# A four-layer graph network on one core: part of the last edge stage's gathers moved to TensorE

## What is computed

```python
def layer_norm(x): return (x - x.mean(-1)) / sqrt(x.var(-1) + 1e-5)
h = maximum(layer_norm(x), 0.0)              # 6250 x 128
h = h @ W
loops = arange(6250)                         # one more self edge per node
src, dst = concat([src, loops]), concat([dst, loops])
deg  = segment_sum(ones, dst)
dinv = rsqrt(deg)
agg  = segment_sum(h[src] * (dinv[src] * dinv[dst])[:, None], dst) + bias
y = relu(layer_norm(agg) * gamma + beta)
out = y + x_before_the_layer
```

## Time and profile before

| | us |
|---|---|
| median of 3 runs | 9720.56 |
| lowest and highest run | 9702.98, 9722.01 |
| span of the profiled execution | 9708.2 |
| fourth edge stage, first to last gather issued | 7626.5 to 9638.9 |

### The profile page before, as it was taken

The page is one execution under the profiler, slowest core; times in us unless marked ns, Lnnn a source line. Parts: engine busy times, 40 slices in busy tenths (PEclk is TensorE's granted clock), DMA queues, the critical chain, the costliest instruction groups (busy, mean ns, idle before and its releaser), DMA issues. The chain is left out here.

```text
span 9708.2 us, 131917 instructions
## 1 busy us (share of the span) xinstructions
PE 5236.0 (54%) x29478; PEld 4578.8 (47%) x29478; DVE 6385.8 (66%) x17574; ACT 1742.2 (18%) x3229; POOL 7212.1 (74%) x6460
## 2 busy tenths in 40 slices
PE   2334343435555555555555588888888444444443
PEld 2333333334445444555545477777777433333333
DVE  4767677776777777666666688888888533333334
ACT  2222222222222222111111111111111200000001
POOL 4777777772888888888888477777777577777775
PEclk6555555556555555555555699999999655555555
DMA  6554554442777667777777422222222212222221
GB/s 154 127 127 116 129 131 117 113 115 65 111 112 111 110 109 110 109 109 111 112 111 111 104 57 56 56 57 56 56 57 56 54 53 53 53 53 53 53 53 52
DMA packets 1095241, 861.72 MB, mean 89 GB/s; under 512 B 408856, under 2 KB 931359, under 8 KB 1094342
## 3 DMA queue, kind: packets, MB, share of 16 engines
q0 software_dynamic: 386880, 427.12, 25.7%
q1 hardware_dynamic: 677244, 314.33, 14.3%
q10 hardware_dynamic: 30652, 115.04, 3.6%
HBM read 706.10 MB, written 149.64 MB: 88 GB/s over the span
## 5 line engine op out<-in xcount | busy, mean ns | idle before, releaser
L1291 POOL DMA_INDIRECT sums<-sumrows,index x1612 | 2520.9, 1564 | 666.2 <-issue 326.6
L675 POOL DMA_INDIRECT rows<-table,index x1612 | 1610.3, 999 | 598.6 <-issue 484.9
L1628 POOL DMA_INDIRECT rows<-table,index x1612 | 1522.6, 945 | 570.5 <-issue 490.7
L1432 POOL DMA_INDIRECT rows<-table,index x1612 | 1546.6, 959 | 512.2 <-issue 393.6
L1686 PE MATMUL psS<-hot,rows 128*128 128x128 f32 x3224 | 824.8, 437 | 1207.8 <-issue 1148.3
L1686 PEld LDWEIGHTS psS<-hot,rows 128*128 128x128 f32 x3224 | 717.8, 328 | 1314.8 <-issue 1270.5
L1259 PE MATMUL psX<-same,hotW 128*128 128x128 f32 x3224 | 810.1, 430 | 975.2 <-DVE hotW L1162 974.6
L1661 DVE TENSOR_TENSOR ACC<-ACC,psS 128x128 f32 x1612 | 465.7, 289 | 1201.6 <-PE psS L1686 1088.3
L1259 PEld LDWEIGHTS psX<-same,hotW 128*128 128x128 f32 x3224 | 698.3, 319 | 1103.1 <-DVE hotW L1162 1102.8
L1268 PE MATMUL psV<-win,mix 128*128 128x129 f32 x3224 | 797.2, 424 | 346.6 <-ACT mix L1225 340.7
L1523 PEld LDWEIGHTS psS<-hot,mid 128*128 128x128 f32 x6448 | 869.9, 196 | 38.1 <-issue 4.9
(11 more groups left out here) (303 smaller groups left out, 9532.9 us busy)
## 6 DMA issues: line engine op xcount, KB each, us to landing
win<-table SPq DMA_DIRECT2D x1612, 64.5 KB
srow<-src_f SPq DMA_DIRECT2D x403, 256.0 KB, 3.6
rows<-table,index POOLq DMA_INDIRECT x4836, 2.5
HN<-rel_f ACTq DMA_DIRECT2D x102, 512.0 KB
relB<-rel_f ACTq DMA_DIRECT2D x102, 512.0 KB, 4.5
er<-limbs SPq DMA_DIRECT2D x1632, 3.0 KB
sums<-sumrows,index POOLq DMA_INDIRECT x1612
ACC<-edge_marks SPq DMA_DIRECT2D x204, 96.0 KB
```

The source lines that it names most:

```text
L675: nc.gpsimd.indirect_dma_start(out=rows[:, r, k, :], out_offset=None, in_=table0[:, :], in_offset=bass.IndirectOffsetOnAxis(ap=index[:, n ...
L1291: nc.gpsimd.indirect_dma_start(out=sums1[u][:, :], in_=sums[:, s, u, :], in_offset=None, compute_op=ALU.add, out_offset=bass.IndirectOffse ...
L1432: nc.gpsimd.indirect_dma_start(out=rows[:, n % R, u, :], out_offset=None, in_=table2[:, :], in_offset=bass.IndirectOffsetOnAxis(ap=index[: ...
L1628: nc.gpsimd.indirect_dma_start(out=rows[:, n % R, u, :], out_offset=None, in_=table3[:, :], in_offset=bass.IndirectOffsetOnAxis(ap=index[: ...
```

## The change

The last BACK = 35 of the 403 groups are no longer gathered by GpSimd. GpSimd gathers the FRONT = 368 groups ahead of them. For the other 35, TensorE selects the source rows out of SBUF by a product with one-hots:

- The rows in `own` are split into three bf16 numbers each (`limbs`, 49 blocks of 128 x 384), high, middle and low part, by ScalarE (L1688, L1691, L1698) and VectorE (`less`, `least`), before ScalarE scales `own`.
- SyncE broadcasts a back group's 512 source numbers to all partitions (`names`), and ScalarE rewrites them as 16-bit integers (`short`).
- For each of the 49 blocks VectorE compares `short` with the block's node numbers (`picks`, L1754): one `tensor_scalar` of 128x512, 16-bit integers to a bf16 one-hot, in a ring of 9 (`pick`).
- TensorE multiplies the one-hots of four tiles by the block's limbs (`gather`, L1827): four matmuls of 384 columns per block, summed over the 49 blocks in four PSUM banks (`psG`). ScalarE copies the sums to `rowsL` (L1710, 128x1536), and TensorE makes the tile sums of a back group with three bf16 matmuls per tile (L1815).
- A back group's 49 blocks are spread over ten front groups (EACH = 10, from group 9 on): 4 or 5 blocks after each group's own matmuls. Group 359 closes the last one; eight front groups follow.
- A group's four sums now share one PSUM bank, three banks in turn, with one semaphore count per group in place of four. `rows` and `hot` move to the free half `ACC[:, 1, :]`.

```diff
-                rows = sb("rows3", [P, R, U, C])
-                hot = sb("hot3", [P, 2, U, P])
-                psS = ps("psS3", [P, 4, 512])
+                BACK, FIRST, EACH = 35, 9, 10
+                FRONT = EDGE_GROUPS - BACK
+                RING, BANKS = 9, 3
+                free = ACC[:, 1, :]
...
+                short = sb("short3", [P, 2, U * P], mybir.dt.int16)
+                pick = sb("pick3", [P, RING, U * P], BF16)
...
                     @block.gpsimd
-                        for n in range(EDGE_GROUPS):
+                        for n in range(FRONT):
                             pool.wait_ge(s_done, n + 1)
...
                     @block.scalar
+                        def leave(m):
+                            act.wait_ge(s_used, TN * (m + 1))
+                            if m:
+                                act.wait_ge(s_sum, turn_back(m - 1) + 1)
+                            nc.scalar.copy(rowsL[:, :, :], psG[:, :, 0:3 * C]).then_inc(s_rowsL, 1)
...
                     @block.vector
+                        def picks(i):
+                            m, own = blocks(i)
+                            for b in own:
+                                at = m * TN + b
+                                if b == 0:
+                                    dve.wait_ge(s_short, m + 1)
+                                if at >= RING:
+                                    dve.wait_ge(s_used, at - RING + 1)
+                                nc.vector.tensor_scalar(pick[:, at % RING, :], short[:, m % 2, :], nodes[:, b:b + 1], None, ALU.is_equal).then_inc(s_pick, 1)
...
+                        for i in range(FRONT):
+                            m = closed(i)
+                            if i + 1 < FRONT:
+                                one_hots(hot[:, (i + 1) % 2, :, :], i + 1, numbers).then_inc(s_hot, 1)
+                            if m is not None:
+                                one_hots(hotB[:, :, :], FRONT + m, numbers).then_inc(s_hotB, 1)
+                            picks(i + 1)
+                            add(turn_of(i), i)
                             dve.sem_inc(s_done, 1)
...
+                            if m is not None:
+                                add(turn_back(m), FRONT + m)
...
                     @block.tensor
+                        def gather(m, b):
...
+                            pe.wait_ge(s_pick, at + 1)
+                            chosen = pick[:, at % RING, :]
+                            for u in range(U):
+                                done = nc.tensor.matmul(psG[:, u, 0:3 * C], chosen[:, u * P:(u + 1) * P], limbs[:, b, :], start=b == 0, stop=b == TN - 1)
+                            done.then_inc(s_used, 1)
+                        for i in range(FRONT):
+                            sums(i)
+                            m = closed(i)
+                            if m is not None:
+                                sums_back(m)
+                            m, own_blocks = blocks(i)
+                            for b in own_blocks:
+                                gather(m, b)
```

More of the change, by code:

```diff
@@ new lines, in gate @@
+                        def gate(g):
+                            for j in range(g * TG, (g + 1) * TG):
+                                done = nc.scalar.activation(hn[:, j, :], hn[:, j, :], ACT.Relu, scale=RSTD[:, j:j + 1])
+                            done.then_inc(s_gate, 1)
+                        shorten(0)
+                        shorten(1)
+                        for m in range(BACK):
+                            if m < steps:
+                                gate(m)
+                            leave(m)
+                            if m + 2 < BACK:
+                                shorten(m + 2)
@@ L1652, in _, with add @@
                         one_hots(hot[:, 0, :, :], 0, numbers).then_inc(s_hot, 1)
[L1654 to L1657, removed]
+                        def add(turn, group):
+                            firsts = windows(dve, group * U)
+                            dve.wait_ge(s_sum, turn + 1)
@@ L1676, in _ @@
-                        for n in range(R * (TN // TG), EDGE_GROUPS):
-                            add(n, n // R, n % R)
+                                nc.vector.tensor_tensor(own, own, psS[:, turn % BANKS, u * P:(u + 1) * P], ALU.add).then_inc(s_free, 1)
+                                dve.wait_ge(s_free, turn * U + (u + 1 + BANKS * U))
+                        def picks(i):
[7 more added lines that the diff above has]
+                                nc.vector.tensor_scalar(pick[:, at % RING, :], short[:, m % 2, :], nodes[:, b:b + 1], None, ALU.is_equal).then_inc(s_pick, 1)
@@ L1679, in _, with sums @@
                     @block.tensor
                     def _(pe):
-                        def sums(n, g, r):
+                        def sums(n):
+                            r, turn = n % R, turn_of(n)
                             pe.wait_ge(s_hot, n + 1)
-                            pe.wait_ge(s_rows[r], 16 * U * g + 16 * U)
+                            pe.wait_ge(s_rows[r], 16 * U * (n // R) + 16 * U)
+                            pe.wait_ge(s_free, turn * U + U)
                             for u in range(U):
-                                pe.wait_ge(s_free, n * U + (u + 1))
-                                nc.tensor.matmul(psS[:, u, 0:P], rows[:, r, u, :], hot[:, r % 2, u, :], start=True, stop=True).then_inc(s_sum, 1)
@@ L1688, in _, with sums_back @@
-                        straight(EDGE_GROUPS, R, sums)
+                                done = nc.tensor.matmul(psS[:, turn % BANKS, u * P:(u + 1) * P], rows[:, r, u, :], hot[:, n % 2, u, :], start=True, stop=True)
+                            done.then_inc(s_sum, 1)
+                        def sums_back(m):
+                            turn = turn_back(m)
+                            pe.wait_ge(s_hotB, m + 1)
+                            pe.wait_ge(s_rowsL, m + 1)
+                            pe.wait_ge(s_free, turn * U + U)
+                            for u in range(U):
+                                for i in range(3):
+                                    done = nc.tensor.matmul(psS[:, turn % BANKS, u * P:(u + 1) * P], rowsL[:, u, i * C:(i + 1) * C], hotB[:, u, :], start=i == 0, stop=i == 2)
+                            done.then_inc(s_sum, 1)
```

118 lines of the change are left out of this document (93 added, 25 removed).

## The result

The changed kernel takes **9554.5 us** (median of 4 runs, 9536.6 to 9560.5), the kernel before in the same sessions 9712.0 (4 runs, 9703.0 to 9722.0). The ratio is 0.9835, with a 95% interval of 0.9821 to 0.9849: 157.5 us less, where 137.5 were forecast. The profiled execution spans 9550.9 us against 9708.2, which is 157.3 less.

A forecast was written before the change was run, and what follows sets the result against it. GpSimd's gathers were taken to bound the last stage: 174.9 us saved less 36.0 and 1.4 gives 137.5, so 9570.7 from the profiled span of 9708.2, plus 12.4 to the runs' median, 9583 us; range 9540 to 9710, holding 0.78.

The forecast's parts named there:

- GpSimd's gathers are the stage.: Last stage: gathers set the pace at 5.00 us per group, so removing 35 groups saves 174.9 us.
- TensorE, 44.0 of 50 us, 88%, at 2.4 GHz.: Last stage: TensorE's matmuls fit within ten front groups' 50.0 us, with the clock up soon after group 9.
- VectorE, 39.4 of 50 us.: Last stage, per ten front groups: 26.4 us for eleven groups plus 13.0 for 49 comparisons at 265 ns; not the bound.
- The comparisons lengthen the gathers by 21 ns each, 36.0 us.: Last stage: 1715 comparisons on VectorE hold GpSimd, at a rate taken from the second stage's scatters beside L1162.
- The lower bound of 0: Last stage: comparisons might lengthen gathers by nothing, if the scatters' excess came from other operations beside them.
- Small edits, 1.4 us.: Last stage: 14 `less` and `least` operations lengthen gathers by 1.0 us; two tiny operations before the first gather add about 0.4.
- The rival "locked out": Gathers beside comparison bursts: at 150 ns lost per comparison, time 9804 us, slower; chance 0.11.
- the upper bound: Last stage: each comparison holds GpSimd for its whole 265 ns, 454 us in all.
- "VectorE becomes the bound": Last stage: comparisons of 0.679 us make ten groups need 59.7 us, time 9887 us; chance 0.05.
- "TensorE becomes the bound": Last stage: unhidden weight loads make ten groups need 56.2 us, time 9764 us; chance 0.06.
- The clock never stayed at 1.2 GHz.: Last stage rival: TensorE's clock stays low, ten groups take 88 us, time 10877 us; chance 0.02.
- The two cost terms: Last stage: gathers lengthened by comparisons, 36.0 us, and by the small added operations, 1.4 us.

The follow-up runs named there:

- two-part run: Changed kernel with two bf16 parts of the table in place of three, 256 columns per matmul, no second subtraction: 9555.7 us, ratio 0.9833.
- the run with eight: Changed kernel with 43 back groups in place of 35, each spread over eight front groups in place of ten, three parts: 9528.0 us, ratio 0.9815.
- The added operations: Kernel before with unread VectorE comparisons added per group: five of 512 16-bit 9729.6 us, one of 2560 9822.6, five of 256 from PSUM 9711.2, five of 512 float32 9833.8.
- the long one: Kernel before with one unread comparison of 2560 16-bit numbers added per group on VectorE: 9822.6 us, ratio 1.0120.

## Why the prediction was right, and where its sizes were off

- *GpSimd's gathers are the stage.* Right. 140 gathers at 1.249 us are 174.9 us, and the stage is 164.6 shorter, so all that the change adds costs 10.3 us of pace where the sum had 37.4.
- *TensorE, 44.0 of 50 us, 88%, at 2.4 GHz.* Right: 438 us of 500 at clock 1.00. Twenty matmuls of 384 columns take 3.41 us with the last one's tail, so weights that change every time don't show. The two-part run shows that the load cost nothing, the run with eight that at 98% it does. Why the tail is 1.4 us shorter stays open; it isn't the clock, which is 0.53 there in both kernels.
- *VectorE, 39.4 of 50 us.* Nearly: 358 us of 500 are busy, 72%. A comparison's median is 347 ns, the forecast's 276 + 69 = 345. In the middle window 490 of them, 388 ns long on average with GpSimd's share in it, fill 164.7 us, so 336 ns each in place of 265: they overlap by 52 ns and not by 80, and they are lengthened. The added operations show the cost of a number: 2560 numbers take 879 ns and 512 take 347, 0.26 ns per number; with float32 512 take 474 ns, 0.25 more per number. The Trainium skill (VectorE: DVE Perf Modes, "Mode 4×_2P — both tricks at once") has four elements per cycle for 16-bit operands; with the 0.96 GHz that the page gives VectorE that is, as an estimate, 0.26 ns per number, and the runs agree.
- *The comparisons lengthen the gathers by 21 ns each, 36.0 us.* This is the term that was mis-sized: 4.6 us, 2.7 ns each, by the kernel without back groups (5.8 us by the changed kernel's own gathers). The 21 ns came from a mean over all scatters of the second stage, where other operations run beside them too, and I gave all of it to L1162. Also the form was wrong: the cost isn't a rate per operation. It depends on which operation runs when a gather starts and on how long that one is, so it was 2.7 ns here, 8.9 ns beside the old kernel's gathers, 47 and 63 ns for float32, 285 for the long one. The lower bound of 0 was much nearer than the rate.
- *Small edits, 1.4 us.* Mis-sized the other way, 5.7 us in the kernel without back groups and 4.5 in the changed one: I took 0.07 us from the one row of a gather beside L1672, which had started when that operation was nearly over; a gather that starts early in one waits 0.87 us. How many do is chance: in the kernel before only one of the gathers beside L1672 and L1675 is over 1.04 us.
- *The rival "locked out".* Gathers are indeed held by a comparison until it ends, but with 16-bit numbers too few are to matter. With float32 numbers GpSimd loses 80 us; the gain would still stand, at 101 ns per comparison it would be gone. The rule of the Trainium skill (SBUF — State Buffer, "Who interferes with whom"), that the two exclude each other for the whole instruction, is borne out for the one instruction under way: the runs have a gather wait to its end. They don't bear out the reading that I set as the upper bound, that each comparison holds GpSimd for its whole length: the wait comes only at certain moments of a gather, and in its second half the comparison is the one that waits. (The 150 ns of this rival was called a value between 101 ns and half of a comparison; half of 265 is 132, so it lies above both.)
- *The other rivals.* "VectorE becomes the bound" was tried with longer comparisons, 9750 in place of 9887, and more of that loss was in longer gathers than in waits for VectorE. "TensorE becomes the bound" needs EACH = 8. The clock never stayed at 1.2 GHz.

The forecast, 9583, was 29 us above the median, inside the range. The two cost terms make 27 us (37.4 against 10.3). The other errors nearly cancel, by luck: the stage began late, which with the shorter tail took 7 us of the gain, and the kernel before ran at 9712.0 in these sessions, 9 us under the 9720.6 that the sum started from.

## What to carry to other kernels

If one engine issues without a pause and two others wait for it, move whole units of its work to them, and read how far you can go from the two busy shares: here TensorE could be filled to 94%, and the next step, to 98%, brought nothing. When VectorE works beside GpSimd's indirect DMAs, what counts is how long a single instruction is whose tensor operands all lie in SBUF, and when it starts against the gathers, not how much of it there is: keep such instructions short, use 16-bit operands, or read one operand from PSUM. A mean over all instances of a pair of engines is no price for one operation; look at the instances that overlap.

## What was unexpected

- One comparison of 2560 numbers costs GpSimd 285 ns, five of 512 together 45 ns, with the same numbers compared.
- Float32 in place of 16-bit numbers makes a comparison 127 ns longer (474 against 347) and the kernel 67 us slower, with VectorE nowhere the bound: the time is in GpSimd's gathers.
- Reading 256 numbers from PSUM takes VectorE longer than 512 16-bit ones from SBUF (475 against 347 ns) and costs GpSimd nothing.
- The first gather of the last stage came at 7616 to 7639 us in kernels with the same earlier stages; that spread is larger than several of the effects above, which is why the stage's own length was needed.
